# Cross-attention and FFN on one core: probabilities and second norm split into fp16 parts and turned by DMA

## What is computed

```
xn = layernorm(x);  q = rope(rms_norm(xn, qw));  k = rope(rms_norm(ctx, kw));  v = ctx
16 heads of 32, 4 key/value heads of 32, causal softmax(q k^T / sqrt(32)) v
x  = x + heads @ w_out.T
y1 = layernorm(x) @ w_up + b_up + lora_up;   w_up: 4 bit numbers with a scale per 64, 512 -> 2048
x  = x + relu(y1) @ w_down + b_down + lora_down;   2048 -> 512, weights likewise
```

## Time and profile before

| what | us |
|---|---|
| median of 3 runs | 566.35 (565.98 to 569.29) |
| the profiled execution | 565.46 |
| its span, first to last instruction | 563.7 |
| PE busy | 513.3 |
| DVE busy | 339.1 |
| ACT busy | 264.4 |
| POOL busy | 206.2 |

### The profile page before, as it was taken

The page is one execution under the profiler, slowest core; times in us unless marked ns, Lnnn a source line. Parts: engine busy times, 40 slices in busy tenths (PEclk is TensorE's granted clock), DMA queues, the critical chain, the costliest instruction groups (busy, mean ns, idle before and its releaser), DMA issues.

```text
span 563.7 us, 12632 instructions
## 1 busy us (share of the span) xinstructions
PE 513.3 (91%) x4968; PEld 366.1 (65%) x4968; DVE 339.1 (60%) x1058; ACT 264.4 (47%) x820; POOL 206.2 (37%) x238
## 2 busy tenths in 40 slices
PE   0257788799999999999999999999999999999997
PEld 0125435475777676767676868686868686868683
DVE  1876535454676767676767676767676767463441
ACT  1456838546453535454545454545454545343110
POOL 3393755802525252525252525252525252222100
PEclk9999659799999999999999999999999999999999
DMA  9960713101203030403031303031302020200000
GB/s 179 296 159 2 212 58 108 38 3 33 58 11 80 12 80 12 80 12 80 14 78 11 81 15 76 13 79 12 79 20 72 10 58 11 57 2 20 2 21 19
DMA packets 59772, 31.89 MB, mean 57 GB/s; under 512 B 48288, under 2 KB 50608, under 8 KB 59664
## 3 DMA queue, kind: packets, MB, share of 16 engines
q1 hardware_dynamic: 56864, 30.58, 22.3%
q10 hardware_dynamic: 2768, 0.34, 0.5%
q0 software_dynamic: 80, 0.16, 0.1%
HBM read 16.39 MB, written 4.19 MB: 37 GB/s over the span
## 4 chain that ended last, share of the span: by engine, by line
PE 82%; POOL 6%; issue 4%; DMA 2%; SPq 2%; DVE 2%; ACT 2%; POOLq 0%; DVEq 0%
PE ff L682 31%; PE ff L697 29%; PE tb L663 7%; PE tb L545 4%; PE tb L652 3%; PE sb L644 2%; DMA big<-in_L_ffn_w_up_q 2%; POOL big L335 2%; PE ff L545 2%; POOL big L332 1%; POOL pr L361 1%; PE kxb L545 1%; PE ff L590 1%; PE ff L605 1%; ACT pr L478 1%
## 5 line engine op out<-in xcount | busy, mean ns | idle before, releaser
L682 PE MATMUL ff<-xnT_hi,wu_hi 128*128 128x128 f16 x1024 | 174.0, 219 | 2.0 <-ACT wd_lo L453 1.1
L361 POOL TENSOR_TENSOR pr<-pr,rinv 128x512 f32<-128x512 f32 x64 | 78.8, 1232 | 264.5 <-DVE rinv L826 264.5
L682 PE MATMUL ff<-xnT_hi,wu_lo 128*128 128x128 f16 x1024 | 173.9, 219 | 0.0
L682 PE MATMUL ff<-xnT_lo,wu_hi 128*128 128x128 f16 x1024 | 173.8, 219 | 0.0
L697 PE MATMUL ff<-wd_hi,x 128*128 128x512 f16 x512 | 152.4, 379 | 0.0
L682 PEld LDWEIGHTS ff<-xnT_hi,wu_hi 128*128 128x128 f16 x1024 | 100.1, 98 | 14.4 <-DVE z L845 11.7
L513 ACT ACTIVATE x<-z 128x512 f16<-128x512 f32 x64 | 40.5, 632 | 133.4 <-DVE z L845 133.4
L682 PEld LDWEIGHTS ff<-xnT_lo,wu_hi 128*128 128x128 f16 x1024 | 100.2, 98 | 0.3
L682 PEld LDWEIGHTS ff<-xnT_hi,wu_lo 128*128 128x128 f16 x1024 | 100.2, 98 | 0.0
L478 ACT ACTIVATE pr<-pr,nmax 128x128 f32<-128x128 f32 x256 | 99.2, 393 | 0.0
L697 PE MATMUL ff<-wd_lo,x 128*128 128x512 f16 x256 | 97.0, 379 | 0.0
(11 more groups left out here) (136 smaller groups left out, 679.2 us busy)
## 6 DMA issues: line engine op xcount, KB each, us to landing
xt<-in_x SPq DMA_DIRECT2D x16, 256.0 KB, 3.0
big<-in_L_ffn_w_up_q SPq DMA_DIRECT2D x4, 1024.0 KB, 13.7
big<-in_L_ffn_w_down_q SPq DMA_DIRECT2D x4, 1024.0 KB, 5.7
out<-y SPq DMA_DIRECT2D x16, 256.0 KB, 2.0
kvt<-in_ctx SPq DMA_DIRECT2D x16, 64.0 KB, 2.5
wd_lo<-in_L_xattn_w_out SPq DMA_DIRECT2D x1, 1024.0 KB, 13.7
wd_hi<-in_L_ffn_w_up_lora_b SPq DMA_DIRECT2D x3, 128.0 KB, 8.2
wd_hi<-in_L_xattn_q_norm_w SPq DMA_DIRECT2D x1, 256.0 KB, 6.3
```

Of the source, the lines that this page charges most:

```text
L361: pool.tensor_tensor(pr[:, m], pr[:, m], rinv[:, p, 4 * m:4 * m + 4].unsqueeze(2).broadcast_to([P, NG, P]), ALU.mult).then_inc(probs, 1)
L682: last = pe.matmul(bank[:, P * h:P * h + P], a[:, m, cols], b[:, p, m, :], start=(h == 0 and m == 0 and i == 0), stop=(m == KC - 1 and i = ...
```

## The change

1. **Probabilities.** Their scale becomes 2^14 over the sum (`scaled_sum` ahead of the reciprocal, one more tiny DVE operation and a wait). ACT writes the high fp16 part (`R_PSPLIT`), POOL the low one (`probabilities_low`, a new POOL operation of 128 x 512 for each group), both into `p3`, which lies in the last quarter of `big`; SP turns them by DMA, 8 blocks a group, into `pT`. The 16 PE turns of a batch and ACT's copies go.
2. **v.** A scale from the norm of the context (a one-column PE product, a tiny DVE and a POOL operation), a high part by ACT and a low one by DVE (128 x 128 each). PV is three rounds of four fp16 products.
3. **Second norm.** ACT and DVE split `xn2` in SBUF into `xn_parts`; SP turns both parts by one DMA of 8 blocks into `xnT`, which is held once. PE's turn and the bank `kxb` go. The calls for the norm stand earlier in the slot: ACT's ahead of the probabilities' parts and the exponentials, DVE's ahead of the residual.
4. **Slots.** Projection, residual and up layer move by one slot, the down layer and result with them.
5. **Staging.** Since `p3` takes a quarter of `big`, three weight groups are staged instead of four: group 3 is loaded inside the loop, and every later load follows a later tile.

```diff
-R_PT = ((8, 15), (9, 16), (10, 17), (11, 18))
-R_PV, R_OSPLIT, R_PROJ, R_X1, R_POW2, R_NORM2, R_TURN2 = (12, 20), (13, 21), (13, 21), (14, 22), (14, 23), (15, 24), (16, 25)
-R_UP, R_DOWN = (18, 26), (22, 30)
+R_PSPLIT = ((8, 15), (9, 16), (10, 17), (11, 18))
+R_VSUM, R_VSPLIT = (5, 12), (6, 14)
+R_PV, R_OSPLIT, R_PROJ, R_X1, R_POW2, R_NORM2 = (13, 20), (14, 21), (14, 22), (15, 23), (15, 23), (16, 24)
+R_UP, R_DOWN = (18, 27), (22, 31)
...
             def load_group(g):
-                if g >= 4:
-                    sp.wait_ge(w_turned, 4 * (g - 3))
+                if g >= W_RING:
+                    sp.wait_ge(w_turned, 4 * (g - W_RING + 1))
...
+                n = at(s, R_NORM2)
+                if n is not None:
+                    sp.wait_ge(xn_high, n + 1)
+                    sp.wait_ge(xn_low, n + 1)
+                    if n > 0:
+                        sp.wait_ge(up_done, 4 * n)
+                    sp.dma_start_transpose(xnT[:], xn_parts[:].rearrange("p a c -> p (a c)")).then_inc(xn2_turned, 16)
...
+                for m in range(NN):
+                    n = at(s, R_PSPLIT[m])
+                    if n is not None:
+                        sp.wait_ge(p_high, 4 * n + m + 1)
+                        sp.wait_ge(p_low, 4 * n + m + 1)
+                        if n > 0:
+                            sp.wait_ge(heads_out, n)
+                        sp.dma_start_transpose(pT[:, m], p3[:, m].rearrange("p g a t -> p (g a t)")).then_inc(p_turned, 16)
-                for g in range(4, 8):
-                    if TILE_AT[4 * (g - 4) + 3] == s:
+                for g in range(W_RING, 8):
+                    if TILE_AT[4 * (g - W_RING) + 3] == s:
                         load_group(g)
...
+            def probabilities_low(s):
+                for m in range(NN):
+                    n = at(s, R_PSPLIT[m])
+                    if n is not None:
+                        pool.wait_ge(p_high, 4 * n + m + 1)
+                        pool.tensor_tensor(p3[:, m, :, 1, :], pr[:, m], p3[:, m, :, 0, :], ALU.subtract).then_inc(p_low, 1)
...
-                    pe.wait_ge(probsT, 4 * n + 4)
-                    for g in range(NG):
-                        d = slice(HD * g, HD * g + HD)
-                        last = pe.matmul(tb[1][d, :], kvt[:, n % RING, d], prT[:, g].rearrange("p n t -> p (n t)"),
-                                         start=True, stop=True)
+                    pe.wait_ge(p_turned, 16 * (4 * n + 4))
+                    pe.wait_ge(v_high, n + 1)
+                    pe.wait_ge(v_low, n + 1)
...
+                    for i, (a, b) in enumerate(((0, 0), (1, 0), (0, 1))):
+                        for g in range(NG):
+                            d = slice(HD * g, HD * g + HD)
+                            last = pe.matmul(tb[1][d, :], v3[:, a, d], pT[:, :, 2 * g + b, :],
+                                             start=(i == 0), stop=(i == 2))
```

More of the change, by code:

```diff
@@ L159, in build @@
         b_in = sem("b_in")
-        wq_in = [sem(f"wq_in{i}") for i in range(4)]
+        wq_in = [sem(f"wq_in{i}") for i in range(W_RING)]
         down_bias_in, b_flat_in = sem("down_bias_in"), sem("b_flat_in")
@@ L595, in weights @@
                 for i in range(4):
-                    last = turn(bank[:, P * i:P * i + P], stage[:, g % 4, i, P * j:P * j + P],
+                    last = turn(bank[:, P * i:P * i + P], stage[:, g % W_RING, i, P * j:P * j + P],
                                 start=False, stop=(i == 3), skip_group_check=True)
@@ L607, in turns @@
             def turns(s):
-                for m in range(NN):
-                    n = at(s, R_PT[m])
-                    if n is not None:
-                        pe.wait_ge(probs, 4 * n + m + 1)
-                        if m >= 2:
-                            pe.wait_ge(probsT, 4 * n + m - 1)
-                        elif n == 0:
-                            pe.wait_ge(wo_low, NN - 1 + m)
-                        elif m == 0:
-                            pe.wait_ge(x1_ready, n)
-                        else:
-                            pe.wait_ge(o_low, n)
-                        for g in range(NG):
-                            last = turn(tb[m % 2][:, P * g:P * g + P], pr[:, m, g, :], start=True, stop=True)
-                        last.then_inc(probs_turned, 1)
-                n = at(s, R_TURN2)
+                n = at(s, R_VSUM)
                 if n is not None:
-                    pe.wait_ge(xn2_ready, n + 1)
+                    pe.wait_ge(ctx_sq, n + 1)
                     if n > 0:
-                        pe.wait_ge(xn_low, n)
-                    for m in range(KC):
-                        last = turn(kxb[:, P * m:P * m + P], xn2[:, P * m:P * m + P], start=True, stop=True)
-                    last.then_inc(xn2_turned, 1)
+                        pe.wait_ge(v_arg_ready, n)
+                    pe.matmul(vb[:, 0:1], ones[:], ssq[:, n % 2:n % 2 + 1], start=True, stop=True).then_inc(v_summed, 1)
             def products(s):
```

149 lines of the change are left out of this document (106 added, 43 removed).

## The result

| | before | after |
|---|---|---|
| time, median of 4 runs | 566.18 us (565.98 to 569.29) | 616.95 us (611.92 to 618.98) |
| span of the profiled execution | 563.7 us | 614.7 us |
| mean granted clock of PE (1 is full speed) | 0.973 | 0.914 |

The changed kernel is slower by a ratio of 1.087 (95% interval 1.079 to 1.095). The forecast was 576 us with a range of 552 to 592: the direction was right, the size was not.

The account below looks back on a forecast made before the run. PE bounds the kernel before; the change makes a ring of waits the bound. Start 163, 13 periods of 28.2 and end 43.8 sum to 573.4 us of span, forecast as 576 us, range 552 to 592.

Parts of the forecast that it names:

- the ring: Loop of waits from one PV to the next through PE, DVE, ACT, POOL, SP and DMA: 28.2 us a period.
- step 1: PE after PV: two up groups, two score groups and the projection, 8.84 us.
- step 5: POOL's own row from power to bias add and low part 1: 5.4 us plus 1.9 held up by DVE, to 17.9.
- step 6: POOL's multiply of group 3, keys, low parts of groups 2 and 3, about 0.5 lost to DVE: to 24.5 us.
- step 7: DMA turn of 8 blocks lands 3.0 us after issue, bounds 2.4 and 4.2; then PV 0.65.
- steps 2 to 4: DVE's residual, mask, low hidden part, inverse sum and norm, then ACT's high parts and exponentials to POOL's multiply: to 17.1 us.
- 3 us of this pass on: At the start, DVE stands 9 us for weight group 3, but only 3 us of that delays later work.
- the second stall: At the start, DVE wants weight group 6 at 87.3 us but it lands at 100; first projection 14 us late.
- The cover of 11.5 us: Before the change, time between the last probabilities leaving POOL and their PV: 11.5 us, which the change spends.
- A price per step: Rival: PV's rounds do not overlap or turns go block by block; period 30.2 or more, 602 us and up; 3%.
- Turns land late: Rival: turns queue with other transfers on one queue and land after 4.2 us; period 29.4, 592 us; 14%.
- PE stays the bound: Rival: parts 3 to 7 are 2.6 us shorter, so PE still bounds; period 25.6, 542 us; 8%.

Follow-up runs that it names:

- e3: The changed kernel with the mask of score group 3 ahead of the residual in DVE's order: 603.42 us.
- e5: The changed kernel with PV, projection, residual, norm, up and down layers and store one slot later against the next batch's attention: 594.11 us.
- e6: The changed kernel with POOL's bias add moved behind the last low part of the next batch: 603.47 us.
- e9: The changed kernel without POOL's low parts of the probabilities (set to zero once; turns and PV's three rounds kept): 585.23 us.
- e14: The changed kernel, same instructions, with four staged weight groups and many steps reordered, lastly centring and sines one slot later: 552.58 us, 0.974 of before.
- e2: The changed kernel with 11 products that nobody reads ahead of PE's wait at PV, from batch 2 on: 610.99 us.
- e1: The changed kernel with four weight groups loaded at the start again instead of three: 602.42 us.
- e7: The kernel before with only the second norm's part of the change, probabilities and PV as before, four weight groups staged: 575.92 us.
- e11: The changed kernel with the loads of x and ctx four slots later in SP's order, behind the probabilities' turns: 615.34 us.

## Why the prediction was right or wrong

Of the 41 us between 576 and 616.95 the start has 20 and the first twelve periods 24; the end has 0.5, and the last period takes 2.5 back.

**Right: which path.** PE stops being the bound and waits at PV for the DMA of the parts, 28.5 us in 14 waits; the steps of the ring are the rows of the chain, and e3, e5, e6 and e9, which each shorten it, each give time back. That cutting it altogether makes PE the bound again is e14's 25.94 us, against "PE alone would need 25.6". PV's three rounds overlap as I took them: 0.76 us where PE is undisturbed, against 0.65. The turn of 8 blocks lands after 3.1 us in the median of all 64, against 3.0 forecast, though not on the path (below). The blocks are not paid one by one: at the Trainium skill's 1309 ns a block (VectorE: DVE Perf Modes, The three transpose paths) the 40 added ones would be 52 us a batch by an estimate from that page, and e14's whole period is half of that.

**Right: the end.** 44.3 us from PV of batch 15, 43.8 forecast.

**Wrong: the size of the ring, 30.17 us for 28.2, 24 us over 12 periods.** The last period came out 2.5 us shorter than forecast, since no next batch stands behind it. The rows of the ring, read in every one of the twelve periods (means, us):

| stretch | forecast | changed kernel | e2 |
|---|---|---|---|
| PV | 0.65 | 0.96 | 0.83 |
| PE to the end of the projection (step 1) | 8.84 | 9.99 | 8.78 |
| to POOL's power (step 2) | 1.78 | 1.94 | 1.94 |
| power to product 3 (step 5) | 7.3 | 7.42 | 7.41 |
| product 3 to the issue of the last turn (step 6) | 6.6 | 6.35 | 6.38 |
| its landing (step 7) | 3.0 | 3.47 | 3.63 |
| landing to PV | 0 | 0.04 | 0.36 |
| sum | 28.2 | 30.17 | 29.34 |

- The term that failed is PE's, in steps 1 and 7: 8.84 + 0.65 was forecast and 10.95 measured. e2, at the full clock, has 9.61, so 1.3 of the 2.0 us that are missing are the clock, which I left out altogether: I forecast a wait of PE of 2 to 3 us and did not ask what it does to what follows. Net, by e2, filling that wait is worth 0.83.
- The landing is the other one. 3.0 us is what the turn of the norm takes and what the median of all turns comes to. The last turn of a batch, the one that PV waits for, took 3.05 to 4.4 us, 3.47 in the mean.
- Power to product 3 came out right in part by luck. I added 1.9 us to POOL's row for DVE and POOL holding each other up. In the period shown that costs 0.8 (bias add 1.68 and low part 1 1.56 for 1.27 each, product 2 1.27 for 1.04, low part 0 1.12 for 1.27); 1.2 us are POOL waiting for DVE's inverse sums, the branch of steps 2 to 4 that I had put 0.8 us ahead of POOL's.
- Product 3 to the issue, step 6, was right. "No bound" was said of SP's sum over a batch; that its queue is a row of a ring, close behind POOL's, I did not see, and e9 shows it.

**Wrong: the start, 182.7 for 163.** The stand of DVE at group 3 came as forecast (8.7 us for 9). The step that failed is "3 us of this pass on" and the second stall: DVE began tile 14 5.6 us later than before, and I looked at groups 3 and 6, but group 5 was the worst, 9.4 us, and put DVE 16.7 us behind at tile 20. The first up group came at 131.7 for 121. e1 prices all these waits at 11.3 us. Of the rest I had expected a gain, 41.3 us from the first up group to PV of batch 2 where it took 51.0: the chain of that stretch already runs through ACT's exponentials, POOL's row and the landing, so the ring bounds batch 2 as well. And PE, with less to do between waits, ran at a mean clock of 0.51 from 57 to 95 us, where it was 0.70 before. How the rest that e1 leaves divides between that clock and the orders is open; without POOL's low parts PV of batch 2 comes 2.8 us earlier (e9), hardly more than the 2.5 us by which two starts of the same code differ.

**The cover of 11.5 us** was counted to PV. For the probabilities' turn on PE it was 2.5 (e7). For the changed kernel the two give the same ring, so this did not move the forecast, but it made me expect 562 for e7.

**The rivals.** "A price per step", 3%, had the nearest number: a period of 30.2 or more and 602 us and up. That is luck. It wanted PV's rounds one after another at 2.6 us or the blocks turned without overlap, and PV took 0.96 and a turn of 8 blocks 3.1. "Turns land late", 592, has a part of the mechanism: the last turn's 3.47 us lie just under the 3.5 from which it was to decide, and make 0.5 of the 2.0 us. "PE stays the bound", 542 at 8%, is what the same arithmetic does in another order: e14.

## What to carry to other kernels

When a step leaves the bounding engine for a longer path over other queues, write the ring down through every engine's program order, the queue that issues the DMAs included, and compare it with the bounding engine's own sum. Here PE was given 2.5 us less to do in a period, the ring was 4.6 us longer than what was left, and the period rose by 2.1. Cutting a ring at one place pays only until the next one closes: single moves gave 2 to 23 us here, and the last, one slot for the centring, 19. If a change makes the bounding engine wait at all, add what its clock does behind the wait. And read more than one period before a reading of the chain is taken for the rule: the last turn waited behind SP in the one shown, and in three of twelve.

## What the runs showed of the hardware

- In the changed kernel a stand of PE of about 2.6 us is followed by a granted clock of 0.61 to 0.69 of full speed, on average, for 5.2 us; with products that nobody reads in its place the clock stays at 1.00 (e2). The length of the stand alone does not decide it. From batch 3 to batch 13 of the changed kernel the clock fell behind each of the ten stands of 1.95 to 3.31 us that PE made at PV and not behind the one of 1.37; in e6 a stand of 3.18 us had no fall behind it, and in e9 one of 1.94 had.
- The issue of a turn of 8 blocks holds SP's queue 1.23 us for the norm, but 1.2 to 2.25 us for the probabilities. The second of a batch, issued right behind the turn of q, took 1.58 us or more in 11 of 12 periods; moving the plain loads away changes nothing that can be measured (e11). Why some of them take longer is not settled.
- Low parts on POOL take 1.15 to 1.61 us for the same shapes. The bias add takes 1.71 us each time while DVE writes the low part of q beside it, and 1.27 each time in e6, where it stands elsewhere. The Trainium skill (GPSIMD Engine Reference, Specifications) says that POOL shares its SBUF interfaces with VectorE and contends with its instructions that have two SBUF inputs; the trace agrees, and what it costs is this spread.
